# Quantized product, stream mixer, attention and gated FFN in one kernel: zero-point term and logits from f16 halves, another order of the front

## What is computed

```python
# first: fake-quantized product of normalised x with the context
q = clip(round(x / s + z), 0, 255); q1 = (q - z) * s      # also for ctx: q2
x = x + q1(layernorm(x)) @ q2(ctx)
# second: 4 streams of 256; its 24 logits per token steer a Sinkhorn (50 iterations) and two softmaxes
x_norm = h * rsqrt(mean(h * h) + eps)                      # h = layernorm(x)
logits = x_norm @ [W_res; W_pre; W_post].T + base          # 16 + 4 + 4
x = x + mix(h; sinkhorn, softmaxes) + branch
# third: attention with Wq, Wk on the context; fourth: FFN of width 2752
```

## Time and profile before

| what | us |
|---|---|
| median of 3 runs | 1218.35 (1216.88 to 1219.41) |
| the profiled execution's own time | 1226.71 |
| its span, first to last instruction | 1224.8 |
| TensorE busy | 1172.4 (96%), granted clock 0.985 in the mean |
| VectorE busy | 780.7 (64%) |
| ScalarE busy | 479.1 (39%) |
| GpSimd busy | 121.7 (10%) |

### The profile page before, as it was taken

How to read it: one execution, slowest core, us unless ns; L and a number is a source line. 1 busy time by engine, 2 the same in 40 slices (tenths; PEclk the granted TensorE clock), 3 DMA queues, 4 the chain that set the end, 5 groups by cost and what they waited for, 6 DMA issues and landing times.

```text
span 1224.8 us, 16343 instructions
## 1 busy us (share of the span) xinstructions
PE 1172.4 (96%) x6362; PEld 579.8 (47%) x6362; DVE 780.7 (64%) x1571; ACT 479.1 (39%) x716; POOL 121.7 (10%) x128
## 2 busy tenths in 40 slices
PE   3989999889999999999999999999999999999998
PEld 2435454554444444554444444444444444444444
DVE  6686788988995267877677676676767652222220
ACT  7773752673244234425443433434334331111110
POOL 4410250036004010200000000000001000000000
PEclk9879999989999999899999999999999999999999
DMA  9530000015032015201112111011111231111300
GB/s 369 207 123 1 1 2 1 1 70 171 2 104 75 7 53 189 77 27 36 69 35 69 42 63 69 36 69 54 51 52 41 81 111 47 47 47 47 127 32 26
DMA packets 26061, 83.57 MB, mean 68 GB/s; under 512 B 3648, under 2 KB 4288, under 8 KB 25984
## 3 DMA queue, kind: packets, MB, share of 16 engines
q1 hardware_dynamic: 25984, 82.53, 19.9%
HBM read 76.22 MB, written 6.29 MB: 67 GB/s over the span
## 4 chain that ended last, share of the span: by engine, by line
PE 72%; DVE 17%; ACT 6%; issue 2%; POOL 1%; DMA 1%; ACTq 0%; SPq 0%; DVEq 0%
PE PAIR L2262 32%; PE PAIR L1896 10%; PE PAIR L1898 10%; PE PAIR L1897 10%; DVE PAIR L1293 3%; DVE LORA L1292 3%; DVE LORA L1294 3%; PE PAIR L1961 2%; DVE X L1340 2%; PE PAIR L2219 2%; PE PAIR L1978 1%; PE PAIR L1969 1%; PE PAIR L2274 1%; PE PAIR L2111 1%; PE PAIR L2002 1%
## 5 line engine op out<-in xcount | busy, mean ns | idle before, releaser
L1896 PE MATMUL PAIR<-POOL 128*128 128x512 f16 x688 | 261.9, 381 | 2.2 <-DVE POOL L1383 2.2
L1898 PE MATMUL PAIR<-POOL 128*128 128x512 f16 x688 | 261.6, 380 | 0.0
L1897 PE MATMUL PAIR<-POOL 128*128 128x512 f16 x688 | 261.5, 380 | 0.0
L2262 PE MATMUL PAIR<-XT,POOL 128*128 128x512 f16 (+1 forms) x1056 | 239.0, 379 | 1.0 <-ACT ST L866 1.0
L2262 PEld LDWEIGHTS PAIR<-XT,POOL 128*128 128x128 f16 (+1 forms) x1056 | 102.6, 98 | 120.5 <-issue 2.5
L2262 PE MATMUL PAIR<-X,POOL 128*128 128x512 f16 (+1 forms) x528 | 121.2, 379 | 0.0
L1898 PEld LDWEIGHTS PAIR<-POOL 128*128 128x128 f16 x688 | 67.2, 98 | 82.2 <-issue 1.3
L1896 PEld LDWEIGHTS PAIR<-POOL 128*128 128x128 f16 x688 | 67.3, 98 | 73.2 <-issue 5.7
L1897 PEld LDWEIGHTS PAIR<-POOL 128*128 128x128 f16 x688 | 67.4, 98 | 65.0 <-issue 1.1
L1511 DVE SCALAR_TENSOR_TENSOR STG<-STG,PAIR 128x1024 f32<-128x1024 f32 (+2 forms) x32 | 28.1, 884 | 92.5 <-PE PAIR L2274 89.1
L900 ACT ACTIVATE POOL<-STG 128x1024 f16<-128x1024 f32 (+2 forms) x32 | 25.0, 788 | 145.3 <-DVE STG L1511 145.3
(11 more groups left out here) (281 smaller groups left out, 1711.1 us busy)
## 6 DMA issues: line engine op xcount, KB each, us to landing
STG<-in_gate_w SPq DMA_DIRECT2D x21, 512.0 KB, 3.5
STG<-in_up_w SPq DMA_DIRECT2D x21, 512.0 KB, 4.2
STG<-in_ctx_t SPq DMA_DIRECT2D x16, 512.0 KB, 3.9
STG<-in_ctx SPq DMA_DIRECT2D x16, 512.0 KB, 4.4
STG<-in_down_w SPq DMA_DIRECT2D x16, 512.0 KB, 3.5
POOL<-in_ctx SPq DMA_DIRECT2D x12, 512.0 KB, 11.2
X<-in_x SPq DMA_DIRECT2D x8, 512.0 KB, 9.7
out_t<-X SPq DMA_DIRECT2D x16, 256.0 KB, 2.9
```

Source lines behind the costliest of these rows:

```text
L1896: e.matmul(dst, l_hi, r_hi, start=first, stop=False)
L1897: e.matmul(dst, l_hi, r_lo, start=False, stop=False)
L1898: return e.matmul(dst, l_lo, r_hi, start=False, stop=last)
L2262: i = e.matmul(dst, blk[:, a_, k, :], src[:, b_, k, :], start=(opens and k == 0 and n == 0), stop=(k == KD // 2 - 1 and n == 2), skip_grou ...
```

## The change

Nine edits, all in the front.

1. The zero-point term is a product of full f16 tiles: `column_parts` (VectorE) and `column_terms` (ScalarE) split the column sums into halves C2, `zero_point_parts` (VectorE, once) writes the factor's halves into four rows of PARTS, and `quant_end` multiplies PARTS by C2.
2. The turned token tile is split into f16 halves too: `second_transposed` (ScalarE) writes the high one, the new `second_lo` (VectorE) the low one, both into XT; the small weights are split once (`small_parts`).
3. The logits come by token: `logits_of` runs 24 f16 products of 24 columns per tile straight into token layout; `logits_across`, `pair_across`, `logit_product`, `pair_logits` and `logit_transpose` go.
4. Nine context tiles (ALONE) need no ScalarE: `clip_q` does scale and offset in one VectorE instruction and both clips in a second. For the other seven it only takes the minimum; rounding moves into GpSimd's `centre_q`.
5. Twelve of the 16 low weight halves go from VectorE to GpSimd (`weight_lo`, ON_VECTOR keeps 0, 2, 4, 7); for each of the twelve ScalarE also scales the fp32 tile in place (`weight_hi`).
6. `row_sums` and the tables of PSUM places change; M begins in PAIR 0.
7. The lists of all engines are written in another order; logits of the first six token tiles come between the products, those of the last two inside the first half of M.
8. The first half of M waits for its weights pair by pair (`weight_done`) rather than for all 16.
9. `second_normal` of the second layer goes behind the exponentials on ScalarE and on into the M stage.

```diff
-        C2 = SMALL[0:1, 0:1024]
+        C2 = SMALL[:, 0:512].bitcast(F16)
+        SMH = SMALL[:, 3264:3264 + KD * NLOG].bitcast(F16).rearrange("p (s k c) -> p s k c", s=2, k=KD)
+        ON_VECTOR = (0, 2, 4, 7)
+        ALONE = (0, 1, 3, 5, 7, 9, 11, 13, 15)
-        PROD_PAIR = (0, 1, 3, 0, 3, 0, 2, 1)
-        HT_PAIR = (0, 1, 3, 0, 3, 0, 2, 1)
-        M_PAIR = (1, 0, 1, 0, 1, 0, 1, 0)
+        PROD_PAIR = (0, 1, 3, 2, 3, 0, 1, 3)
+        HT_PAIR = (0, 1, 3, 2, 3, 0, 1, 3)
+        M_PAIR = (0, 1, 0, 1, 0, 1, 0, 1)
...
             def centre_q(n):
-                e.tensor_scalar(Q2[n // KP][:, n % KP, :], FSTAGE[n], 1.0, -(MAGIC + QHALF), ALU.mult,
+                e.tensor_scalar(Q2[n // KP][:, n % KP, :], FSTAGE[n], MAGIC, -(MAGIC + QHALF), ALU.add,
                                 ALU.add).then_inc(q2_ok, 1)
+            def weight_lo(i):
+                e.wait_ge(w_hi, i + 1)
+                e.tensor_tensor(W2[i][:, 1, :], FSTAGE[i + AHEAD], W2[i][:, 0, :], ALU.subtract).then_inc(wp_lo, 1)
...
+            for i in range(2 * KD):
+                if i not in ON_VECTOR:
+                    weight_lo(i)
             for g in range(NT):
                 branch_sum(g)
...
             def weight_hi(i):
                 e.wait_ge(front_in[i + AHEAD], 32 if i + AHEAD < N_W else 16)
                 e.wait_ge(q2_ok, i + 1)
                 if i >= AHEAD:
-                    e.wait_ge(w_lo, i - AHEAD + 1)
-                e.activation(W2[i][:, 0, :], FSTAGE[i + AHEAD], ACT.Copy, scale=WS).then_inc(w_hi, 1)
+                    weight_done(e, i - AHEAD)
+                st = FSTAGE[i + AHEAD]
+                last = e.activation(W2[i][:, 0, :], st, ACT.Copy, scale=WS)
+                if i not in ON_VECTOR:
+                    last = e.activation(st, st, ACT.Copy, scale=WS)
+                last.then_inc(w_hi, 1)
...
             def clip_q(n):
-                e.wait_ge(q_relu, n + 1)
-                e.tensor_scalar(FSTAGE[n], FSTAGE[n], 255.0, MAGIC, ALU.min, ALU.add).then_inc(q_clip, 1)
+                if n in ALONE:
+                    e.wait_ge(front_in[n], 16)
+                    chain(e.tensor_scalar(FSTAGE[n], FSTAGE[n], col(RQ2), z2, ALU.mult, ALU.add))
+                    e.tensor_scalar(FSTAGE[n], FSTAGE[n], 0.0, 255.0, ALU.max, ALU.min).then_inc(q_clip, 1)
+                else:
+                    e.wait_ge(q_relu, n + 1 - sum(i < n for i in ALONE))
+                    e.tensor_scalar(FSTAGE[n], FSTAGE[n], 255.0, None, ALU.min).then_inc(q_clip, 1)
...
+            def second_lo(g):
+                t = g % BT
+                e.wait_ge(ht_hi, g + 1)
+                e.scalar_tensor_tensor(XT[:, 0, 1, :, t * P:(t + 1) * P],
+                                       PAIR[HT_PAIR[g]][:, :].rearrange("p (k t) -> p k t", k=KD), HS,
+                                       XT[:, 0, 0, :, t * P:(t + 1) * P], ALU.mult, ALU.subtract).then_inc(ht_lo, 1)
...
             def quant_end(g):
...
-                    i = e.matmul(PAIR[PROD_PAIR[g]][:, hs], ONESF[0:1, :], C2[:, hs], start=False, stop=True)
+                    i = e.matmul(PAIR[PROD_PAIR[g]][:, hs], PARTS[:, :], C2[:, hs], start=False, stop=True)
...
-            def logit_product():
+            def logits_of(g):
...
                 for k in range(KD):
-                    i = e.matmul(PAIR[2][0:NLOG, 0:S], SMF[:, k, :], HTT[:, k, :], start=(k == 0), stop=(k == KD - 1))
+                    for n, (x_, w_) in enumerate(((0, 0), (0, 1), (1, 0))):
+                        i = e.matmul(dst, XT[:, 0, x_, k, ts], SMH[:, w_, k, :], start=(t == 0 and k == 0 and n == 0),
+                                     stop=(k == KD - 1 and n == 2), skip_group_check=True)
                 i.then_inc(lg_p, 1)
```

More of the change, by code:

```diff
@@ L961, in _ @@
+            weight_hi(3)
             norm_root(0, 4)
-            for i in range(3, 6):
-                weight_hi(i)
-            column_terms(1)
+            weight_hi(4)
+            weight_hi(5)
             weight_hi(6)
+            take_logits(0)
+            second_transposed(4)
+            weight_hi(7)
+            weight_hi(8)
+            weight_hi(9)
+            second_transposed(5)
+            weight_hi(10)
+            weight_hi(11)
+            second_transposed(6)
+            weight_hi(12)
@@ L975, in _ @@
-            second_normal(3)
-            for i in range(11, 15):
-                weight_hi(i)
-            logits_across()
-            weight_hi(15)
-            second_transposed(4)
-            take_logits(0)
-            second_transposed(5)
-            pair_across(0)
-            second_transposed(6)
-            second_transposed(7)
-            norm_root(4, 8)
-            root(RX2, RX)
-            pair_across(2)
-            take_logits(1)
-            sinkhorn_start()
-            branch_streams(0)
@@ L992, in _ @@
             branch_streams(1)
-            for g in range(BT, NT):
-                second_normal(g)
             for n in range(2 * KD):
@@ L1004, in _ @@
                     branch_input(g)
+                    if g + 3 < NT:
+                        second_normal(g + 3)
                     if g + 2 < NT:
@@ new lines, in zero_point_parts @@
+            def zero_point_parts():
+                e.wait_ge(ones_ok, 1)
+                chain(e.memset(PARTS[:, :], 0.0))
+                for r in range(0, P, 32):
+                    e.tensor_scalar(PARTS[r:r + 1, :], ONESF[r:r + 1, :], SM[r:r + 1, NZD1:NZD1 + 1], 4.0, ALU.mult, ALU.mult)
+                chain(e.tensor_scalar(OMGI[:, 0:P], ONESF[:, :], col(NZD1), 4.0, ALU.mult, ALU.mult))
+                for r in (32, 96):
+                    i = e.tensor_tensor(PARTS[r:r + 1, :], OMGI[r:r + 1, 0:P], PARTS[r:r + 1, :], ALU.subtract)
+                chain(i)
@@ L1625, in _ @@
+            column_parts(1)
+            second_lo(3)
             product_stats(2)
-            add_product(3)
             product_stats(3)
-            weight_lo(0)
             norm_ask(0, 4)
-            weight_lo(1)
             weight_lo(2)
             norm_rest(0, 4)
-            for i in range(3, 7):
-                weight_lo(i)
+            weight_lo(4)
             add_product(4)
+            product_stats(4)
+            second_lo(4)
+            add_product(5)
             weight_lo(7)
-            product_stats(4)
@@ L1638, in _ @@
-            weight_lo(8)
-            add_product(5)
-            weight_lo(9)
             product_stats(5)
-            for i in range(10, 2 * KD):
-                weight_lo(i)
+            second_lo(5)
+            add_product(6)
+            product_stats(6)
+            second_lo(6)
+            add_product(7)
+            product_stats(7)
+            norm_ask(4, 8)
             bias_operands()
             gate_terms()
-            add_product(6)
-            add_product(7)
-            product_stats(6)
@@ L1649, in _ @@
-            product_stats(7)
-            norm_ask(4, 8)
+            second_lo(7)
             norm_rest(4, 8)
```

318 lines of the change are left out of this document (159 added, 159 removed).

## The result

The changed kernel takes 1247.13 us (median of 4 runs, 1246.62 to 1248.12) against 1218.88 us before (4 runs): ratio 1.023, interval 1.0206 to 1.0254. It is **slower by 28 us**; the forecast was 1204.3, in a range of 1196 to 1214. The profiled execution took 1247.06 us, span 1245.3. What was predicted of TensorE, and nearly the length of the second half, came about; what ruined it is an engine that the working hardly mentions.

A forecast was written before the change was run, and what follows sets the result against it. TensorE was taken to bound the front's second half. The first half unchanged, the second 47.2 us in place of 61.3, puts the exponential 14.1 us earlier: 1218.35 - 14.1 = 1204.3 us, range 1196 to 1214.

The forecast's parts named there:

- Stage A: Front up to the last centred context tile: VectorE's added work fills its idle time, the end stays at 66.1 us.
- the clip with two pointers: VectorE clip with two per-partition operands, in no row: taken as 0.96 us, between 0.69 and 1.22; ends -6 and +9.
- 17.0 idle us with 16.1 of work: VectorE up to 66.1 us: 8.7 + 6.4 + 2.6 - 1.6 = 16.1 us added, against 51.4 - 34.4 = 17.0 idle.
- the 0.96 I took: VectorE's clips before 66.1 us: 0.96 us each, the mean over both groups of clips in the rows.
- rival (b): VectorE becomes the bound of the front up to 66.1 us: clips at 1.22, +9 us, time 1213.4; chance 0.15.
- Stage B: From 66.1 us to the Sinkhorn's first exponential: 47.2 us in place of 61.3; TensorE no longer the bound, ScalarE longest.
- the 2.125 of the earlier trace: GpSimd's low weight halves after 66.1 us: twelve at 2.125 us, 25.5 us where it did nothing before.
- VectorE was put at 34.3 us: VectorE from 66.1 us to the exponential: 41.2 - 14.6 for low halves + 7.7 for added instructions = 34.3 us.
- 11.9 were put for waits and clock: ScalarE after 66.1 us: 0.7 us for last column sums, 7.7 of waits, 3.5 added for TensorE's clock.
- I take the difference off both sides: Whole kernel: median 8.4 us below the profiled execution; this difference left out of the gain, so 1218.35 - 14.1.
- the 14.1 us in stage B: Gain at the exponential that starts the Sinkhorn: at 113.3 us instead of 127.4, 14.1 us earlier.
- (d): Slower: TensorE stays at 1.2 GHz between 66.1 us and the exponential, 7 us late, 1225.4; chance 0.08.

The follow-up runs named there:

- run 1: Changed kernel with centre_q back as product and add, the rounding constant added again in VectorE's clips: 1215.87 us, ratio 0.9965 to the kernel before.
- run 2: Kernel before with centre_q alone changed to two adds, clip_q keeping only its minimum: 1240.42 us, ratio 1.0167.
- Run 5: run 1 with five context tiles in place of nine quantized by VectorE alone: 1213.89 us, ratio 0.9935 to the kernel before.
- run 6: run 1 with all sixteen low weight halves on GpSimd: 1213.56 us, ratio 0.9947 to the kernel before.
- run 7: run 1 with both five tiles alone on VectorE and all sixteen low halves on GpSimd: 1212.52 us, ratio 0.9935 to the kernel before.
- run 8: run 7 with PARTS written by GpSimd before its first tile: 1211.09 us, ratio 0.9901 to the kernel before.
- Run 4: Kernel before, unchanged, profiled a second time: 1222.43 us, span 1220.5.
- run 10: run 7 with all low weight halves back on VectorE: 1217.98 us, ratio 0.996 to the kernel before.

## Why the prediction was wrong

**The step that failed: "Stage A, up to 66.1: forecast no change."** Its costing went through VectorE, ScalarE and TensorE. Of GpSimd it had "rounding moves into `centre_q`" in the list of edits, and no price: the operand list changed from (1.0, product; add) to (add; add), the count and the shape did not, and the 1.04 us of the earlier trace rows was silently carried over. The form was in no row and should have got bounds like the clip with two pointers got. Measured: 16 x 2.55 = 40.9 us more on an engine with 51.4 - 27.2 = 24.2 us idle in the stage, nearly all of it in waits between tiles. Only 9.7 of these were filled, 14.5 stayed idle, and stage A grew by 32.3 us; runs 1 and 2 show it undone and done alone.

**Mis-sized in the same stage: VectorE.** I filled 17.0 idle us with 16.1 of work and left the end where it was. Run 1 shows 55.3 us of work up to the last `centre_q`. Before, up to the same mark:

```profile
12.80:66.10 53.30, 39.19 (x175) 18.00 (x174) 36.23 (x60) 45.18 (x44) 29.14 (x24) 0.94 0.75 278
```

So 19.1 us were added, 3.0 more than the sum. The clips were nearly right: in run 1 the 33 take 32.0 us, 0.97 each against the 0.96 I took, though single ones run from 0.67 to 1.53. (The 0.96 had left out four clips of 0.80 in the same list before; all 24 give 0.94.) The groups of run 1:

```profile
L1208 DVE TENSOR_SCALAR POOL<-POOL 128x1024 f32<-128x1024 f32 x7 | 8.5, 1208 | 0.2
L1207 DVE TENSOR_SCALAR POOL<-POOL,SM 128x1024 f32<-128x1024 f32 x7 | 7.1, 1011 | 0.0
L1230 DVE TENSOR_SCALAR PARTS<-ONESF,SM 1x128 f16<-1x128 f32 x4 | 1.9, 484 | 0.1
```

PARTS took 2.9 us in run 1 where I estimated 1.5, `small_parts` 1.4 where I had nothing. Four small instructions of the roots took 0.69 to 1.03 us in place of 0.16, 3.1 us in all, each beside a GpSimd instruction that starts within 0.4 us of it; against that, more statistics moved behind the stage than the one set of the sum. An engine at 55.3 of 57.5 us has hardly room, so VectorE as the bound, rival (b), was what remained once the form was repaired, by another road than the 1.22-us clips it named: 4.1 us later, inside its bound of 9. Run 5 agrees: with less for VectorE to do the stage ends 2.6 us earlier.

**Stage B: right on TensorE, wrong on who ends last.** TensorE stopped being the bound: it was put at 38.2 us of work there and did 38.1. GpSimd's low halves, 2.1 to 2.5 us in the means of their groups, bear out the 2.125 of the earlier trace rows. Forecast 47.2, measured 49.4, and 48.0 to 48.6 in runs 1 and 5 to 8. That the length came so near is partly luck: the forecast's path to it was another. Wrong is who ends last, and the term behind it: VectorE was put at 34.3 us and did 39.3, in run 1 43.0, and the exponential waits for its logits. The sum took VectorE's other instructions at the pace they had with GpSimd idle, but beside the halves three of them took 5.4 us more. ScalarE, put at 35.3, did 33.9 and waited 15.5 us, where 11.9 were put for waits and clock.

**The gain was measured from a bad base.** "I take the difference off both sides" put the 8.4 us between the profiled execution and the median into no stage. Run 4 shows an execution 4.3 us faster, all of it in the front, where TensorE ran less at 1.2 GHz. It is one execution, itself 1.8 us above the median beside it; but against it about 4 of the 14.1 us in stage B were never there to be won. The sum against run 4: 57.3 - 48.3 = 9.0 us from stage B, less 4.5 in stage A (70.26 - 65.79), is 4.6 us at the exponential, and run 1 is 4.6 us below before's median (2 to 7 by its interval). That fits the repaired kernel.

**What held after the front.** From the exponential to the Sinkhorn's end it is 95.3 to 95.9 us in every profile here, and in the changed kernel M's first half ended closer behind the exponential than before (1.5 us, 2.7 before). What follows the Sinkhorn's end, which the edits leave alone, took 996.6 to 1004.1 us in the kernels profiled. Here too TensorE, after a wait, runs for a few us at 1.2 GHz in some profiles and not in others. 270 us after the Sinkhorn's end, in the kernel before (us, busy, granted clock):

```profile
492.70:494.70 2.00, 2.00 (x6) 0.50 0.00 0
```

The same place in run 1:

```profile
485.90:487.90 2.00, 2.00 (x11) 1.00 0.00 0
```

From the Sinkhorn's end to the program's end it was 1002.1 us in the first, 999.4 in the second and 996.6 in run 2, which shows no such spell at this place nor in the 16 to 36 us after the Sinkhorn's end, where the other two have some. Over the runs of the kernel before beside run 1, the time falls as the mean granted clock rises (1216.73 us at 0.994, 1224.97 at 0.985). That fits such spells as the source of the 8-us width of runs of one kernel; what a single one costs, and that nothing else adds to it, isn't shown. No edit here is aimed at them.

**The rivals.** (d), slower, came out in sign and not in mechanism: TensorE's clock in stage B was 0.85, as before (0.86). The longest clips were 1.53 us, the mean 0.97. The rule of the Trainium skill ("SBUF — State Buffer", section "Who interferes with whom"), taken to its end, had 1.73 for each; run 1 shows clips that last 0.7 us longer beside GpSimd, so less than its whole instruction, and others that don't. It is VectorE's small instructions that came near the whole of one: up to 1.8 us longer beside the halves of 2.1 to 2.3 us. What decided was in none of the cases, and the 0.08 given to "slower" was the chance of one mechanism, not of an edit that I had not priced.

Put together: 1247.1 - 1204.3 = 42.8 us, of which 31.3 are the form of `centre_q` (run 1), 4.1 VectorE in stage A and 1.1 stage B (both run 1), 4.3 the base (run 4); 2.0 are left, about what the median of before itself moved between chips (1218.35 and 1220.48). The first is shown by an edit undone and done alone; the others are read from single profiles.

## What to carry to other kernels

Price every instruction whose operand list changes, also when its count, shape and engine stay: on GpSimd the choice of the two operations alone moved one from 1.05 to 3.6 us. Where no row shows the new form, give it bounds, and ask of each engine in turn what it gains, even of one that is idle for half of the stage. Work moved to an idle engine can still slow the engine it was taken from: three small instructions of VectorE ahead of the exponential took 5.4 us longer beside the halves that GpSimd had taken over, though by run 10 the move still paid. Before a gain is taken from a profile, look whether that execution is typical: a stage that holds disturbed time shows more to win than there is.

## What was not expected of the hardware

GpSimd's elementwise instruction with constants (TENSOR_SCALAR) on 128x1024 elements, f32 to bf16, takes 1.05 us as product and add in either order (up to 1.5 beside VectorE), and 2.77 to 4.6 us in the six other ways tried, a lone add or subtract among them. VectorE's clips take 0.7 to 0.8 us or 1.4 to 1.5, none between in run 1's stage A, 0.97 in the mean. An instruction of VectorE on 128x4 elements took 1.95 us beside a GpSimd half of 2.13 us, and 0.16 in run 10 with GpSimd idle.
